# A four-layer graph network on one core: the first loads regrouped and halved, the last batch's mask moved from TensorE to VectorE

## The reference

```
x = layernorm(x + relu(softmax(leaky(s_i + t_j) masked by adj) @ H))       # layer 0: one head, H = x @ W
x = layernorm(x + elu(8 heads of the same, 16 wide))                       # layer 1
x = layernorm(x + relu(LN(adj/deg @ x @ Wr + x @ Ws.T + b)*gamma + beta))  # layer 2: only relation 1 occurs in adj
x = layernorm(x + 4 heads of softmax(Wh @ Wh.T / sqrt(32) masked by adj) @ Wh)  # layer 3
```

## Time and profile before

| | before |
|---|---|
| median of 3 runs | 2694.97 us (2694.97 to 2699.35) |
| profiled execution, its own time | 2698.47 us |
| its span, first to last instruction | 2696.7 us |
| PE busy | 2387.9 us, 89% |
| DVE busy | 2158.0 us, 80% |
| ACT busy | 1966.9 us, 73% |
| mean granted clock of PE | 0.949 |

### The profile page before, as it was taken

How to read it: one execution, slowest core, us unless ns; L and a number is a source line. 1 busy time by engine, 2 the same in 40 slices (tenths; PEclk the granted TensorE clock), 3 DMA queues, 4 the chain that set the end, 5 groups by cost and what they waited for, 6 DMA issues and landing times.

```text
span 2696.7 us, 56998 instructions
## 1 busy us (share of the span) xinstructions
PE 2387.9 (89%) x23921; PEld 1584.9 (59%) x23921; DVE 2158.0 (80%) x4075; ACT 1966.9 (73%) x2193; POOL 183.8 (7%) x103
## 2 busy tenths in 40 slices
PE   3567998989899898989989899998989999898967
PEld 3557566575756557575565757656485655657331
DVE  2688788897978889797888978888897978989642
ACT  2657787777778777777877777787777887777724
POOL 0000000010100001010000100001010000101000
PEclk9778999999999998999999999999989999899989
DMA  5504041220414122041412304141130413101000
GB/s 121 118 24 119 25 119 33 72 72 28 100 33 119 32 71 72 16 112 33 111 40 58 86 9 119 32 111 40 46 98 9 119 32 80 39 27 41 9 9 8
DMA packets 190369, 164.42 MB, mean 61 GB/s; under 512 B 136608, under 2 KB 170528, under 8 KB 189088
## 3 DMA queue, kind: packets, MB, share of 16 engines
q1 hardware_dynamic: 188832, 127.22, 16.9%
q0 software_dynamic: 1280, 33.56, 6.1%
HBM read 151.78 MB, written 42.53 MB: 72 GB/s over the span
## 4 chain that ended last, share of the span: by engine, by line
PE 51%; DVE 27%; ACT 11%; issue 9%; SPq 1%; DMA 0%; POOL 0%; ACTq 0%; DVEq 0%; POOLq 0%
PE kp L748 12%; PE kp L731 9%; PE fp L574 9%; PE fp L633 7%; DVE weight L1245 7%; ACT ramp L921 6%; PE kp L724 6%; ACT weight L968 2%; DVE x L1081 2%; DVE vh L1253 2%; DVE ramp L1231 2%; DVE bstat L1062 1%; PE fp L525 1%; PE fp L649 1%; DVE yb L1081 1%
## 5 line engine op out<-in xcount | busy, mean ns | idle before, releaser
L921 ACT ACTIVATE ramp<-s1row,tbig 128x1024 bf16<-128x1024 f32 x864 | 926.6, 1142 | 119.1 <-DVE weight L1245 112.9
L1245 DVE TENSOR_TENSOR weight<-ramp,AT 128x2048 bf16<-128x2048 bf16 x512 | 613.5, 1219 | 155.7 <-ACT ramp L921 142.3
L968 ACT ACTIVATE weight<-kp,shift 128x1024 f32<-128x1024 f32 x512 | 543.1, 1111 | 227.6 <-PE kp L731 224.0
L633 PE MATMUL fp<-vh_parts,weight 128*128 128x102 bf16 x8192 | 456.6, 217 | 83.1 <-DVE weight L1245 71.4
L633 PEld LDWEIGHTS fp<-vh_parts,weight 128*128 128x128 bf16 x8192 | 417.3, 102 | 181.8 <-DVE weight L1245 111.1
L748 PE MATMUL kp<-weight,w 128*33 128x512 f32 x2048 | 489.4, 599 | 6.6 <-ACT weight L968 5.7
L731 PE MATMUL kp<-shared 32*128 32x512 f32 x2048 | 296.8, 649 | 3.1 <-ACT weight L968 3.1
L748 PEld LDWEIGHTS kp<-weight,w 128*33 128x33 f32 x2048 | 97.6, 110 | 298.1 <-issue 239.9
L574 PEld LDWEIGHTS fp<-h,weight 128*128 128x128 f32 x2048 | 239.2, 197 | 50.4 <-issue 36.1
L574 PE MATMUL fp<-h,weight 128*128 128x129 f32 x2048 | 247.8, 282 | 16.0 <-DVE weight L1158 16.0
L1380 DVE SCALAR_TENSOR_TENSOR weight<-AT,weight 128x1024 f32<-128x1024 bf16 x160 | 188.7, 1221 | 68.4 <-ACT weight L968 67.6
(11 more groups left out here) (182 smaller groups left out, 2627.4 us busy)
## 6 DMA issues: line engine op xcount, KB each, us to landing
s1row<-s_rows_dram SPq DMA_DIRECT2D x128, 512.0 KB, 5.0
adj_bf_dram<-in_adj_dram POOLq DMA_DIRECT2D x16, 2048.0 KB, 14.1
x<-in_x_dram SPq DMA_DIRECT2D x16, 512.0 KB, 7.3
xfT<-s_row_dram SPq DMA_DIRECT2D x16, 512.0 KB, 5.3
out_dram<-elu SPq DMA_DIRECT2D x16, 512.0 KB, 3.2
s_rows_dram<-weight SPq DMA_DIRECT2D x16, 32.0 KB
weight<-in_L_gnn_a_dram SPq DMA_DIRECT2D x2, 128.0 KB, 9.0
AT<-adj_bf_dram SPq DMA_TRANSPOSE x16, 11.1
```

Source lines behind the costliest of these rows:

```text
L633: last = pe.matmul(fp[:, 1 + t // 4, col:col + 2 * PARTS * C1], edges[:, u % B_RING, t * P:(t + 1) * P], vh_parts[:, jt, h, :, :, :].rearr ...
L921: act.activation(ramp[:, u % R_RING, :], s1row[:, h % S_RING, :], ACT.Relu, bias=tbig1[:, jt, h:h + 1], scale=BIG).then_inc(ramp_ready.sem, 1)
L968: act.activation(weight3[:, w % P_RING, :], kp[:, 1 + 2 * (w % 2):3 + 2 * (w % 2), :].rearrange("p a n -> p (a n)"), ACT.Exp, bias=shift3[ ...
L1245: dve.tensor_tensor(edges[:, u % B_RING:u % B_RING + 2, :], ramp[:, u % R_RING:u % R_RING + 2, :], AT[:, third, jt:jt + 2, :], ALU.min).th ...
```

## The change

It has two parts. At the start, the weight loads fall into three groups with a semaphore each. SP issues only layer 0's two loads, then the first `x`. POOL waits for `x` and casts the first adjacency in two halves of 512 rows; SP waits for the first half and transposes it, issues five loads (layer 1's, `self_w`, the bias, layer 3's), waits for the whole cast and transposes the second half, and issues the last three (layer 2's). DVE's preparation is split: `prepare_first` makes layer 0's two columns before anything else, and `prepare_rest` stands ahead of `layer0_z(0)`. PE's transpose of `self_w` moves behind the transposition of batch 0's maxima, into another bank. The cast of batch 1 waits in addition for batch 0's source row to have landed. At the end, all 16 pairs of the last batch are masked by DVE, and PE leaves out the mask products of all of them; the other batches keep pairs 10 to 14.

```diff
+    def masks(b):
+        return tuple(range(PAIR_UNITS)) if b == NB - 1 else MASKED
...
-                      ramps=[3, 9, 18, 32, 49], most0=32, maximum0=50, masked3=[90, 95, 103, 109, 110])
+                      ramps=[3, 9, 18, 32, 49], most0=32, maximum0=50, masked3=[90, 90, 90, 90, 90, 90, 90, 90, 90,
+                      90, 90, 95, 103, 109, 110, 110])
...
-            for dst, src in loads:
-                sp.dma_start(dst, src).then_inc(w_loaded, 16)
+            def load(dst, src, done):
+                sp.dma_start(dst, src).then_inc(done, 16)
...
+            load(rhs0[:, 0:D], L0_gnn_W, w0_loaded)
+            load(a0_row, L0_gnn_a.rearrange("(k u) o -> o k u", k=2).broadcast_to([P, 2, D]), w0_loaded)
+            load_x(0)
+            sp.wait_ge(a_first_half, 16)
+            sp.dma_start_transpose(AT[:, 0, :, 0:HALF], adj_dram[0:HALF, :]).then_inc(at_first_half, 16)
+            load(self_w, L2_gnn_self_w, w1_loaded)
+            load(rhs1[:, 0:D].rearrange("p (h o) -> p h o", h=H1), L1_gnn_W.rearrange("h f o -> f h o"), w1_loaded)
+            load(a1_row, L1_gnn_a.rearrange("h k o -> o h k").broadcast_to([P, H1, 2 * O1]), w1_loaded)
+            load(bias2, to_all(L2_gnn_self_b), w1_loaded)
+            load(rhs3[:].rearrange("p (h o) -> p h o", h=H3), L3_gnn_W.rearrange("h f o -> f h o"), w1_loaded)
+            sp.wait_ge(a_loaded.sem, a_loaded.of(0))
+            sp.dma_start_transpose(AT[:, 0, :, HALF:N], adj_dram[HALF:N, :]).then_inc(at_ready.sem, 16)
+            load(rhs2[:, 0:D], L2_gnn_rel_weights[1], w2_loaded)
+            load(gamma2[:], to_all(L2_gnn_ln_gamma), w2_loaded)
+            load(beta2[:], to_all(L2_gnn_ln_beta), w2_loaded)
             def period(r, f, k, m, n):
-                if n is not None:
+                if n is not None and n > 0:
                     load_x(n)
                     turn_adjacency(n, (r + 1) % 3)
...
+                if b == 1:
+                    pool.wait_ge(at_first_half, 16)
+                    pool.wait_ge(s0_loaded.sem, s0_loaded.of(0))
...
-            load_adjacency(0)
+            pool.wait_ge(x_loaded.sem, x_loaded.of(0))
+            first = adj[bass.ds(0, 1)].rearrange("b i j -> (b i) j")
+            pool.dma_start(adj_dram[0:HALF, :], first[0:HALF, :]).then_inc(a_first_half, 16)
+            pool.dma_start(adj_dram[HALF:N, :], first[HALF:N, :]).then_inc(a_loaded.sem, 16)
...
-                    for x in range(2 if v not in MASKED else 0):
+                    for x in range(0 if v in masks(b) else 2):
...
-            pe.wait_ge(w_loaded, 160)
+            def turn_self_weights():
+                pe.wait_ge(w1_loaded, 80)
+                pe.transpose(kp[:, 4, 0:P], self_w, ident[:]).then_inc(self_turned, 1)
             pe.wait_ge(consts_made, 3)
-            pe.transpose(fp[:, 0, 0:P], self_w, ident[:]).then_inc(self_turned, 1)
-            pe.wait_ge(weights_ready, 1)
...
                         layer0_turn_maxima(n)
+                        if n == 0:
+                            turn_self_weights()
...
-            act.wait_ge(weights_ready, 1)
...
+            def prepare_first():
+                dve.memset(st0[:], 0.0)
+                dve.memset(h0[:, :, D:D + 1], 1.0)
+                dve.wait_ge(w0_loaded, 32)
                 for k in range(2):
                     dve.tensor_tensor(w_tmp, rhs0[:, 0:D], a0_row[:, k, :], ALU.mult).then_inc(step.sem, 1)
                     dve.wait_ge(step.sem, step.step())
...
+                last.then_inc(weights0_ready, 1)
+            def prepare_rest():
+                dve.wait_ge(weights0_ready, 1)
+                dve.wait_ge(w1_loaded, 80)
+                dve.wait_ge(consts_made, 3)
...
-            prepare_weights()
+            prepare_first()
...
                     if n is not None and s == ON_DVE["z0"]:
+                        if n == 0:
+                            prepare_rest()
                         layer0_z(n)
...
-                    for i, v in enumerate(MASKED):
-                        if k is not None and s == ON_DVE["masked3"][i]:
+                    for v in range(PAIR_UNITS):
+                        if k is not None and v in masks(k) and s == ON_DVE["masked3"][v]:
                             layer3_masked(k, (r + 2) % 3, v)
```

More of the change, by code:

```diff
@@ L254, in tiles @@
             return slice(GROUPS[g][0], GROUPS[g][-1] + 1)
-        w_loaded = sem("w_loaded")
+        w0_loaded = sem("w0_loaded")
+        w1_loaded = sem("w1_loaded")
+        w2_loaded = sem("w2_loaded")
+        a_first_half = sem("a_first_half")
+        at_first_half = sem("at_first_half")
         consts_made = sem("consts_made")
         self_turned = sem("self_turned")
+        weights0_ready = sem("weights0_ready")
         weights_ready = sem("weights_ready")
@@ L403, in _, with to_all @@
         def _(sp):
[L404 to L415, removed]
-            for dst, src in loads:
-                sp.dma_start(dst, src).then_inc(w_loaded, 16)
+            def load(dst, src, done):
+                sp.dma_start(dst, src).then_inc(done, 16)
+            def to_all(row):
+                return row.rearrange("(a d) -> a d", a=1).broadcast_to([P, D])
             def load_x(b):
@@ L550, in layer0_project @@
                 else:
+                    if b == 0:
+                        pe.wait_ge(weights0_ready, 1)
                     pe.wait_ge(x0T_ready.sem, x0T_ready.of(b))
@@ L567, in layer0_unit @@
                 if jt == 0:
+                    if b == 0:
+                        pe.wait_ge(at_first_half, 16)
                     pe.wait_ge(at_ready.sem, at_ready.of(b))
@@ L583, in layer1_project @@
             def layer1_project(b):
+                if b == 0:
+                    pe.wait_ge(weights_ready, 1)
                 pe.wait_ge(x1T_ready.sem, x1T_ready.of(b))
@@ L646, in layer2_project @@
             def layer2_project(b):
+                if b == 0:
+                    pe.wait_ge(w2_loaded, 48)
                 pe.wait_ge(x2T_ready.sem, x2T_ready.of(b))
@@ L731, in layer3_scores @@
                         last = pe.matmul(kp[:, 1 + 2 * (w % 2) + x, :], mine[:, jt * P:(jt + 1) * P],
-                                         mine[:, n * HALF:(n + 1) * HALF], start=v in MASKED, stop=True,
+                                         mine[:, n * HALF:(n + 1) * HALF], start=v in masks(b), stop=True,
                                          skip_group_check=True)
@@ L738, in layer3_values @@
                 g, J = v // 4, v % 4
-                if v in MASKED:
-                    pe.wait_ge(masked3_ready.sem, masked3_ready.of(b, 2 * MASKED.index(v) + 2))
+                if v in masks(b):
+                    pe.wait_ge(masked3_ready.sem, masked3_ready.of(b, 2 * masks(b).index(v) + 2))
                 else:
@@ L1083, in normalise @@
                 last.then_inc(done, 1)
-            def prepare_weights():
-                dve.wait_ge(w_loaded, 160)
-                dve.wait_ge(consts_made, 3)
-                step = Steps(dve_setup)
-                step.begin(0)
+            step = Steps(dve_setup)
+            step.begin(0)
+            def prepare_first():
+                dve.memset(st0[:], 0.0)
+                dve.memset(h0[:, :, D:D + 1], 1.0)
+                dve.wait_ge(w0_loaded, 32)
                 for k in range(2):
@@ L1092, in prepare_weights @@
                     dve.wait_ge(step.sem, step.step())
-                    dve.tensor_reduce(rhs0[:, D + k:D + k + 1], w_tmp, AX_X, ALU.add).then_inc(step.sem, 1)
-                    dve.wait_ge(step.sem, step.step())
+                    last = dve.tensor_reduce(rhs0[:, D + k:D + k + 1], w_tmp, AX_X, ALU.add)
+                    if k == 0:
+                        last.then_inc(step.sem, 1)
+                        dve.wait_ge(step.sem, step.step())
+                last.then_inc(weights0_ready, 1)
[3 more added lines that the diff above has]
+                dve.wait_ge(consts_made, 3)
                 for k in range(2):
@@ L1122, in prepare_weights @@
                 dve.memset(h1[:, :, :, O1:C1], 1.0)
-                dve.memset(h0[:, :, D:D + 1], 1.0)
                 dve.memset(y2_hi[:, :, D:D + 1], 1.0)
@@ L1126, in prepare_weights @@
                 dve.wait_ge(self_turned, 1)
-                dve.tensor_copy(rhs2[:, D:2 * D], fp[:, 0, 0:P]).then_inc(weights_ready, 1)
+                dve.tensor_copy(rhs2[:, D:2 * D], kp[:, 4, 0:P]).then_inc(weights_ready, 1)
             def layer0_top(b):
@@ L1154, in layer0_unit @@
                 if jt == 0:
+                    if b == 0:
+                        dve.wait_ge(at_first_half, 16)
                     dve.wait_ge(at_ready.sem, at_ready.of(b))
@@ L1328, in layer2_affine @@
             def layer2_affine(b):
+                if b == 0:
+                    dve.wait_ge(w2_loaded, 48)
                 dve.wait_ge(brstd_ready.sem, brstd_ready.of(b, 1))
```

4 lines of the change are left out of this document (2 added, 2 removed).

## The result

The changed kernel takes 2682.68 us, the median of 6 runs (2678.74 to 2685.26), against 2695.70 us for the kernel before (6 runs, 2694.39 to 2700.74). The ratio is 0.9946, with a 95% interval of 0.9933 to 0.9958: 13.0 us less. The profiled execution took 2682.63 us, 15.84 less than the profiled one of before. The prediction was 2680.0, a gain of 14.7.

What follows compares the result with a forecast made beforehand. PE is busy 89%, but the edit touches only two edges: the head, waiting on DMA, and the tail, with PE full. Head 10.5 plus tail 4.2 makes 14.7 us, from 2694.97 to 2680.3; predicted 2680, range 2672 to 2689.

Steps and rivals of the forecast that it cites:

- The head: Start of the program: SP's queue up to the store of `row0` comes last; gain 10.5 us, bounds 2.4 and 18.
- The one disputed term: Head: first half transpose, issued beside the cast's second half, is held up by it; SP free at 22.5 us.
- The free transpose: Rival, head: the cast doesn't hold up the transpose; head gives up to 18 us, total 2673 us; chance 12%.
- Halving gives nothing: Rival, head: halves gain nothing and load groups stall; SP free at 36.8 us, total 2685 us; chance 14%.
- The stall of 9.88 us: Head, SP's weight loads: one issue took 9.88 us before; a rival added 6 us for such a stall.
- `prepare_rest` comes last: Rival, head: a late second group ends DVE's preparation past the row; costs 1 to 4 us, 2683 us; chance 6%.
- The hold on the second cast: Head, `row0` from store to landing: batch 1's cast moves behind `s0_loaded(0)`; 5.9 us taken, a gain of 0.9.
- The delayed cast: Batch 1's cast: starts at 38 us, lands by 52, its transpose is issued some 83: 30 us of cover.
- The tail: Last batch's layer 3: mask products leave PE for DVE; gain 4.2 us, bounds 3.2 and 5.0.
- PE has slack: Tail: where DVE masks, ACT's exponentials set 3.49 us a pair; ten such steps gain 5.0 us.
- the 0.8 for pair 15: Tail, last pair: DVE's two last masks have nothing to hide behind; 8.28 us instead of 7.51, 0.8 lost.
- the rival of the falling clock: Rival, tail: gaps in PE lower its clock, 2.2 us more per pair; 15 pairs give 2713 us; chance 3%.

Runs made afterwards that it cites:

- the whole cast: The changed kernel, but the first adjacency is cast and transposed in one piece, before both later groups of loads: 2686.44 us, ratio 0.9962.
- the cast at once: The changed kernel, but POOL casts the first adjacency without waiting for `x`: 2680.79 us, ratio 0.9940.
- the tail alone: The kernel before, with only the edit that lets DVE mask all pairs of the last batch: 2694.61 us, ratio 0.9988.
- the row first alone: The changed kernel, but `row0` is stored and spread right after the first half transpose; second transpose, loads, `self_w` turn and `prepare_rest` come later: 2676.11 us, ratio 0.9921.
- the head alone: The changed kernel with only its edits at the start; the last batch keeps its mask products on PE: 2685.06 us, ratio 0.9957.

## Why the prediction was right, and where not

**The head, by its own steps.** The prediction had SP's queue as what comes last, and the trace has it step by step:

| Step | predicted, us | measured, us |
|---|---|---|
| `x` landed | 6.2 | 6.53 |
| row ready | 18.5 | 17.6 |
| first half of the cast landed | 13.8 | 14.77 |
| SP free after the first transpose | 22.5 | 21.52 |
| second group issued | 26.0 | 24.18 |
| SP free after the second transpose | 30.5 | 29.05 |
| store of `row0` | 31.8 | 30.67 |
| from the store to the landing | 5.9 | 6.0 |
| gain at `layer0_z` | 10.5 | 11.5 |

The first half came 1.0 later than forecast, 7.94 us after the issue, close to the upper bound of 8.5. Two terms more than made it up: the first transpose held SP for 6.75 us, not the 8.7 from 13.8 to 22.5, and the second group took 2.6, not 3.5. The one disputed term, the transpose beside the cast, is right in kind and 2 us too long: half of a whole one is 3.8, and SP is free at 21.5, some 1.7 us after the second half is over at 19.7 (issued at 7.52, landed 12.2 us later). Of the 962 packets that the hardware queue got through from 15 to 20 us, the profile has none before 18 us, 226 from there to 19 and 736 from 19 to 20. The last 16 large packets of the cast (0.52 MB) stand between 16 and 17, some 2.5 us each by their share of the engines (254.4% of that 1 us). So the transpose got next to nothing through while those ran, and went on beside the cast's last small ones. The free transpose, at SP free 17.6, did not happen.

The fall of the first group's wait gave what it should: PE starts at 6.66 us. Between `layer0_z` and the first `rstd` another 0.9 us went, since the 128 products of layer 0 took 16.29 us in place of 17.17. The forecast had nothing there, and rightly: in the kernel with the tail edit alone, whose head is before's, they took 16.14. Over all the kernels they took 15.9 to 17.2 us, so this 0.9 is no gain of the edit that the runs can show.

**The rivals in the head.** *Halving gives nothing* was half right: the halves give 2.5 us at `layer0_z` by one trace each. The medians point the same way (0.9962 with the whole cast against 0.9946), but their intervals overlap. The stall of 9.88 us of the earlier trace rows didn't come back: no load of the change takes over 0.58 to issue. The Trainium skill, "DMA: Bandwidth & Descriptors", section "Rules for kernel authors", says that two transfers to disjoint halves of the partitions serialize and aren't worth it. The halves here are rows in DRAM, so it is not quite the page's case. The transfers gained nothing by themselves: both halves of the cast had landed at 19.7, the whole one at 19.8. The halves paid all the same, as other issues stood behind the first transpose in the queue. The measurement decides. *`prepare_rest` comes last* was given 6% with a late landing of the second group. In the change the preparation was over 2.8 us early, and the forecast had 3; the whole cast and the cast at once both turned it into what comes last, by 0.3 and about 1 us. The cover was as thin as it was priced.

**The hold on the second cast** was under-priced in a way that a sum against before can't show. It was entered at 0.9 us, the difference to the way from store to landing of before. Against the change without it, it is worth 9.7. The head's 10.5 us were only there with it: store at 31 us and cast at 32 would have met.

**The middle** stayed: 2525.38 us against 2526.33, within what equal code differs by here. The delayed cast had 30 us of cover and used none of it that shows.

**The tail** is the term that was mis-sized: 2.5 us, not 4.2, and below the lower bound of 3.2. The step that failed is "PE has slack", at a granted clock of 1.00. It holds for 14 of 15 steps at 3.49 us. For pair 0 it doesn't: the values run at the lower level, 3.61 us where 1.91 was meant, and the step to pair 2 takes 4.84 instead of 3.49, 1.35 us lost. The turn back took 2.80 instead of 2.42, another 0.4. Together: 4.2 - 1.35 - 0.4 = 2.5. The pace and the 0.8 for pair 15 were right. The five pairs of the earlier trace rows bore out the steady state only; they follow ten pairs of a full PE, whereas pair 0 follows a stretch at 0.71. So the rival of the falling clock came true in one place, at 1.35 us, and not in 15 pairs at 2.2 each. That it hangs on the missing products, pair 0's above all, is shown by the kernels above (3.61, 2.82, 1.91); all nine traces without pair 0's products have the dip, at 2.82 to 3.61, and none of the three with them. The Trainium skill, "TensorE: Matmul & The Clock Gate", section "A second HAM failure mode: psum-queue depth-cycling", has the clock swing on short gaps between groups; here gaps of 0.2 to 0.5 us in every pair left it at 1.00 for 38 us. The turn back's 0.4 isn't settled: it took 2.80, 2.78, 2.82 and 2.70 in the change, the tail alone and the kernels with pairs 1 and 15 or 0, 1 and 15 on PE, 2.75 or 2.76 with the whole cast, the row first alone and the cast at once, and 2.42 or 2.43 in before, the head alone, with pair 15 alone on PE, and in the kernel with the second cast not held, which masks all pairs on DVE.

**The sum.** 11.5 + 0.9 + 2.5, and 0.95 in the middle, are the 15.84 us of the profiled executions; 13.0 stands in the medians, 14.7 was forecast. The head came out 1.9 better, 0.9 of it no work of the edit, the tail 1.7 worse. The mechanism was right, but that the sum came so close is in part luck: its errors cancel.

## What to carry to other kernels

When loads are regrouped, write down the whole queue of the issuing engine with a time for each entry, and look for a result that is ready long before its turn: the row lay for 13 us behind loads that nobody needed yet, and putting it first was worth another 7.2 us on top of the change by the traces (medians 0.9921 against 0.9946, intervals that just touch). A transfer that moves earlier may meet another that it used to miss; price a wait against the new schedule, not against the old. Where products leave TensorE, look at what runs just before them: here the first pair lost 1.35 us of what the steady ones gained.

## What the runs showed of the hardware that was not expected

Beside the int32 to bf16 cast of GpSimd's queue, a 512 KB load slows far more than by half: `x` from 4.80 to 15.87 us, the row from 3.73 to 12.95. Each landed only when the cast was over, 1.5 and 0.7 us behind it (17.60 after 16.1, 46.34 after 45.6). In the 13 us of the slow row load, this is what the queues moved, in the kernel with the second cast not held:

```profile
q0 software_dynamic: 80, 2.10, 80.8%
q1 hardware_dynamic: 179, 0.54, 10.7%
```

By these rows a packet of the cast's queue is 26 KB (2.10 MB in 80), one of the hardware queue 3 KB (0.54 MB in 179). Over the whole 13 us the counts are not equal. But while the cast's large packets run, they are nearly so: 53 of the cast and 40 of the hardware queue from 33.4 to 42 us, and 47 and 46 from 9 to 13 us in the kernel with the cast at once. Together with the 42 packets against 42 of the earlier trace rows this looks like turns by packets, not by bytes; no kernel here varied the packets' size, so it is argued, not shown. The Trainium skill, "DMA: Bandwidth & Descriptors", section "Queues, rings and completion order", says that an engine takes turns between its queues a packet at a time; these near-equal counts agree, but don't prove it.

A transposing DMA of half an adjacency landed in 8.8 us beside the cast and in 6.8 after it, while its issue held SP for 6.75 and 4.82.
